# A new order of work inside the pipelined loop of a two-layer gated cross-attention kernel

## The reference

```
x += tanh(g_x[0]) * attention_A(layernorm(x), ctx, mask)   # one head of 256 over ctx, 1601 rows; softmax over 1601
x += tanh(g_f[0]) * mixture_B(layernorm(x))                # router picks 4 of 16 heads of 64; self-attention over 512
x += tanh(g_x[1]) * attention_C(layernorm(x), ctx, mask)   # 16 heads of 16 over the same 1601 rows of ctx
x += tanh(g_f[1]) * experts_D(layernorm(x))                # each row goes to 1 of 8 experts, 256 -> 1024 -> 256
```

## Time and profile before

| | |
|---|---|
| median of 3 runs | 3290.82 us (3289.27 to 3303.54) |
| the profiled execution, its own time | 3308.77 us |
| its span, first to last instruction | 3307.0 us |
| PE busy | 2877.2 us, 87% |
| DVE busy | 1719.2 us, 52% |
| ACT busy | 1459.8 us, 44% |
| granted clock of PE, mean | 0.937 |

### The profile page before, as it was taken

How to read it: one execution, slowest core, us unless ns; L and a number is a source line. 1 busy time by engine, 2 the same in 40 slices (tenths; PEclk the granted TensorE clock), 3 DMA queues, 4 the chain that set the end, 5 groups by cost and what they waited for, 6 DMA issues and landing times.

```text
span 3307.0 us, 38212 instructions
## 1 busy us (share of the span) xinstructions
PE 2877.2 (87%) x13236; PEld 1331.4 (40%) x13236; DVE 1719.2 (52%) x4156; ACT 1459.8 (44%) x2794; POOL 316.6 (10%) x364
## 2 busy tenths in 40 slices
PE   5758988998899888998899889988998888859997
PEld 3423423353334333443344334433343322148886
DVE  1335556556555656555655565555555676621111
ACT  2122454545454555445454545454545555612221
POOL 0110001010100100010101010101010000012221
PEclk7878998999899999999999999998999999969999
DMA  4124212322232214220323032303221121026665
GB/s 156 54 70 110 56 34 77 88 61 50 70 94 55 64 36 119 55 74 28 99 69 80 16 119 62 82 20 119 63 63 33 53 55 36 8 90 220 219 208 175
DMA packets 190687, 267.58 MB, mean 81 GB/s; under 512 B 47813, under 2 KB 159661, under 8 KB 190358
## 3 DMA queue, kind: packets, MB, share of 16 engines
q1 hardware_dynamic: 173084, 189.97, 21.3%
q0 software_dynamic: 17408, 75.13, 6.7%
HBM read 203.24 MB, written 65.61 MB: 81 GB/s over the span
## 4 chain that ended last, share of the span: by engine, by line
PE 72%; DVE 15%; ACT 5%; issue 4%; SPq 3%; DMA 1%; POOL 0%; ACTq 0%; POOLq 0%; DVEq 0%
PE PS L1233 12%; PE PS L1184 10%; DVE mxC L1655 9%; PE PS L1216 7%; PE PS L953 6%; PE PS L929 5%; PE PS L1344 5%; PE PS L1355 5%; PE PS L1019 2%; PE PS L1099 2%; PE PS L1036 2%; PE PS L1029 2%; PE PS L976 2%; DVE nmB L1494 1%; PE PS L940 1%
## 5 line engine op out<-in xcount | busy, mean ns | idle before, releaser
L860 ACT ACTIVATE reg<-PS 128x512 f32<-128x512 f32 (+1 forms) x1664 | 970.3, 598 | 1205.2 <-PE PS L1216 1201.9
L1655 DVE TENSOR_REDUCE mxC<-PS 128x1 f32<-128x400 f32 (+1 forms) x2048 | 1090.1, 569 | 752.9 <-PE PS L1184 743.2
L1184 PE MATMUL PS<-reg 96*128 96x400 bf16 (+1 forms) x2048 | 693.0, 351 | 176.5 <-DVE mxC L1655 155.7
L1216 PE MATMUL PS<-reg 99*128 99x512 bf16 (+1 forms) x1664 | 642.5, 396 | 32.5 <-ACT reg L860 27.1
L1184 PEld LDWEIGHTS PS<-reg 96*128 96x128 bf16 x2048 | 203.1, 99 | 725.0 <-DVE mxC L1655 598.9
L1233 PE MATMUL PS<-reg 128*17 128x512 f32 (+1 forms) x3328 | 461.8, 628 | 0.0
L1216 PEld LDWEIGHTS PS<-reg 99*128 99x128 bf16 (+1 forms) x1664 | 165.6, 102 | 348.5 <-ACT reg L860 159.1
L929 PE MATMUL PS<-reg 128*128 128x512 f32 (+1 forms) x512 | 206.0, 526 | 1.2 <-ACT reg L756 0.7
L883 ACT ACTIVATE reg<-PS,reg 128x256 f32<-128x256 f32 x184 | 77.3, 471 | 271.0 <-PE PS L1344 271.0
L953 PE MATMUL PS<-reg 128*128 128x512 f32 (+1 forms) x416 | 193.1, 598 | 0.4 <-ACT reg L728 0.4
L1344 PE MATMUL PS<-reg 128*128 128x256 f32 x736 | 165.4, 382 | 0.9 <-DVE reg L1815 0.9
(11 more groups left out here) (202 smaller groups left out, 2614.7 us busy)
## 6 DMA issues: line engine op xcount, KB each, us to landing
reg<-in_D_W SPq DMA_DIRECT2D x46, 1024.0 KB, 7.5
reg<-in_A_mask POOLq DMA_DIRECT2D x32, 800.5 KB, 4.8
dramK<-reg SPq DMA_DIRECT2D x144, 100.0 KB
dramV<-reg SPq DMA_DIRECT2D x48, 272.0 KB, 2.1
reg<-in_ctxT POOLq DMA_DIRECT2D x8, 1601.0 KB, 8.3
reg<-in_ctx POOLq DMA_DIRECT2D x8, 1536.0 KB, 8.1
dramQ<-reg SPq DMA_DIRECT2D x96, 128.0 KB
reg<-dramQ SPq DMA_DIRECT2D x32, 384.0 KB, 5.8
```

The lines of the kernel that those rows point to most:

```text
L860: act.activation(pr[u % RING][0:r, :], PS[0:r, s_bank(g, v), :], ACT.Exp).then_inc(a_expC, 1)
L1184: last = mm(PS[:, bank, 0:w], qs[(NG * bb + g) % 3][0:ROWS, h, t * P:(t + 1) * P], ks[g % 2][0:ROWS, h, c0:c0 + w], start=True, stop=True)
L1216: last = mm(PS[0:r, bank, :], ks[g % 2][0:STK, h, c * P:c * P + r], qs[(NG * b + g) % 3][0:STK, h, :], start=True, stop=not with_mask)
L1655: v.tensor_reduce(mxC[:, h, t, j:j + 1], PS[:, MB[i % 2], 0:M_CH[j][1]], AX.X, ALU.max).then_inc(v_mx, 1)
```

## The change

It alters no arithmetic and no number of matmuls, and moves the work between steps and banks.

1. A table, `PIECES`, one digit for each step of a group, says how many pieces (0 to 3) stand in it. `chunks` reads it.
2. The pieces of a step no longer stand first and last: after `scores_t`, after `values_c` of v >= 7, inside many filler parts (between the two halves of a projection) and after each part, `piece()` issues the next one, if there is one left. DVE does the same between its parts.
3. `transpose_m` writes to the maxima bank `MB[0]`. `scores_t` no longer waits for `copy_rows`, and the first piece of the next group does.
4. The projections of keys and of values of C alternate, one of each every four steps, from step 34 to 62 in opposite banks; half of the keys had stood at steps 124 to 133.
5. In stage B, `max_b`, `exp_b` and `normalise` take one tile a step, the pitch of `score_b` goes from four steps to five, and `weigh_b` is split over two steps.
6. In stage A, the layer norm and `turn_x` (`U_XA`) go from 151 to 77, `project_qg` to 136, the scores from 164 to 141, and all sixteen transposes end at step 196 (four stood in steps 2 to 8 of the next period). `weigh_a` issues one matmul a step in 26 steps, where it issued three in every second step.
7. The queries of C (`U_QC`) go from 136 and 138 to 150 and 152; other parts move by a few steps. The transfers move with them.

```diff
-FIRST, LAST = (3, 3, 3, 5), (43, 43, 43, 44)
-U_PV = [10 + 2 * i for i in range(10)]
-U_O1, U_O2, U_OA = (11, 13), (15, 17), (30, 32)
-U_XD, U_GATE = (31, 33), 36
-U_V = [34, 36, 38, 40, 42, 45, 47]
-U_XB, U_RL = (44, 46), 50
-U_K = [52, 56, 60, 64, 124, 127, 130, 133]
-U_QB, U_KB, U_VB = (70, 71), (73, 74), (76, 77)
-U_SB = [80 + 4 * k + 2 * (k >= 4) for k in range(8)]
-U_TB = [U_SB[i // 2] + (5, 7)[i % 2] for i in range(16)]
-U_PVB, U_OB, U_XC, U_QC = (101, 119), (121, 122), (132, 134), (136, 138)
-U_XA, U_QG = (151, 153), (155, 157)
-U_S = [164, 166, 168, 170, 174, 176, 178, 180, 187, 189, 191, 193, 199, 201, 203, 205]
-U_T = [175, 177, 179, 181, 185, 188, 190, 192, 198, 200, 202, 204, 2, 4, 6, 8]
+PIECES = ("0002213322232323311211210113121301010112001300000000",
+          "0003003312230132102331233323111111031002110100000000",
+          "0001001211031002110222133323330021330113312300000000",
+          "0000000022222213311121322213311121221122111220000000")
+U_O1, U_O2, U_LD, U_XD, U_GATE = (7, 10), (13, 16), 18, (27, 30), 33
+U_OA, U_LB, U_XB, U_RL = (29, 31), 34, (43, 46), 50
+U_K, U_V = [34 + 4 * i for i in range(8)], [35 + 4 * i for i in range(7)]
+U_QB, U_KB, U_VB = (66, 68), (70, 72), (74, 76)
+U_LA, U_XA = 68, (77, 80)
+U_SB = [79 + 5 * k + 3 * (k >= 4) for k in range(8)]
+U_TB = [U_SB[i // 2] + 6 + 2 * (i % 2) for i in range(16)]
+U_PVB, U_OB, U_LC = (U_SB[3] + 11, U_SB[7] + 11), (132, 133), 135
+U_QG, U_XC, U_QC = (136, 138), (143, 146), (150, 152)
+U_S = [141, 144, 147, 149] + [154 + 12 * t + d for t in range(3) for d in (0, 3, 6, 8)]
+U_T = [U_S[4 * t + 3] + 4 + 2 * j for t in range(QT) for j in range(4)]
+U_PV = [199 + 13 * c // 10 for c in range(2 * CT)]
...
 def chunks(g, v):
-    first, last = FIRST[g], LAST[g]
-    upto = [min(max(-(-NSC * (w - first + 1) // (last - first + 1)), 0), NSC) for w in (v - 1, v)]
+    upto = [sum(int(d) for d in PIECES[g][:w]) for w in (v, v + 1)]
     return range(*upto)
...
-            def project_qg(n, LA, m):
+            def project_qg(n, LA, m, piece):
...
                     last = mm(PS[:, FB[m], :], gA[:, k, m * P:(m + 1) * P], xT[:, k, :],
                               start=k == 0, stop=k == KD - 1)
+                    if k == 0:
+                        piece()
...
             def scores_c(bb, g, i, with_mask):
                 h, t, j = chunk(i)
                 if i == 0:
+                    past(pe, a_mrow, NG * bb + g)
...
-                    last = tr(PS[0:3 * GH, bank, t * P // 2:(t + 1) * P // 2].bitcast(BF16),
+                    last = tr(PS[0:3 * GH, MB[0], t * P // 2:(t + 1) * P // 2].bitcast(BF16),
...
-                if v == MT[g]:
-                    pe.wait_ge(a_expC, U)
-                elif v == MT[g] + 1 and (g < NG - 1 or ab):
-                    pe.wait_ge(a_mrow, NG * b + g + 2)
-                else:
-                    past(pe, a_expC, U - 1)
+                past(pe, a_expC, U - 1)
...
+                todo = iter(ahead)
+                def piece():
+                    for i in todo:
+                        scores_c(nb, ng, i, with_mask)
+                        break
+                piece()
...
-                    if u == 153:
+                    if u == U_QC[1] + 8:
                         store_q(n, 1)
...
-            def max_b(n, k):
-                for h in range(2):
-                    i = 2 * k + h
+            def max_b(n, i):
...
-                for k in range(8):
-                    if u == U_SB[k] + 1:
-                        max_b(n, k)
-                    if u == U_SB[k] + 3:
-                        normalise(n, k)
+                for i in range(16):
+                    if u == U_SB[i // 2] + 1 + i % 2:
+                        max_b(n, i)
+                        piece()
+                    if u == U_SB[i // 2] + 4 + i % 2:
+                        normalise(n, i)
+                        piece()
```

More of the change, by code:

```diff
@@ L830, in start_next @@
                         evac_qg(m, k)
-                for i in range(12):
+                for i in range(16):
                     if u == U_T[i] + 1:
@@ L836, in start_next, with copy_rows @@
                         exp_a(m, t)
[L838 removed]
+            def copy_rows(bb, g):
                 act.wait_ge(pe_mT, NG * bb + g + 1)
[L840 removed]
+                act.activation(mrow[:], PS[0:3 * GH, MB[0], 0:S // 2].bitcast(BF16), ACT.Copy).then_inc(a_mrow, 1)
             def evac_o(bb, g):
@@ L893, in _, with nothing @@
             FB = (F0, F1)
+            def nothing():
+                pass
             pe.wait_ge(ld["a"], 16)
@@ L950, in weigh_a, with out_a @@
                     pe.wait_ge(v_ttr, 16 * n + 16)
-                for c in range(3 * j, min(3 * j + 3, CT)):
-                    r = rows(c)
-                    last = mm(PS[:, FB[m], :], ctxN[0:r, c, m * P:(m + 1) * P], ptA[0:r, c, :],
-                              start=c == 0, stop=c == CT - 1)
-                if j == 4:
+                r = rows(c)
+                last = mm(PS[:, FB[m], :], ctxN[0:r, c, m * P:(m + 1) * P], ptA[0:r, c, :],
+                          start=c == 0, stop=c == CT - 1)
+                if c == CT - 1:
                     last.then_inc(pe_otA, 1)
-            def out_a(n, j):
+            def out_a(n, j, piece):
                 pe.wait_ge(a_otA, 2 * n + 2)
@@ L985, in route, with project_b @@
                 last.then_inc(pe_rl, 1)
-            def project_b(n, m, which):
+            def project_b(n, m, which, piece):
                 if which == 0:
@@ L1030, in turn_b, with weigh_b @@
                 last.then_inc(pe_tB, 1)
-            def weigh_b(n, p):
-                pe.wait_ge(a_ptB, 16 * n + 8 * (p + 1))
-                for k in range(QT):
+            def weigh_b(n, p, half):
+                if half == 0:
+                    pe.wait_ge(a_ptB, 16 * n + 8 * (p + 1))
+                for k in (2 * half, 2 * half + 1):
                     for h in range(2):
@@ L1037, in weigh_b, with out_b @@
                                   ptB[h][:, k, :], start=k == 0, stop=k == QT - 1)
-                last.then_inc(pe_pvB, 1)
-            def out_b(n, j):
+                if half:
+                    last.then_inc(pe_pvB, 1)
+            def out_b(n, j, piece):
                 pe.wait_ge(v_otB, 2 * n + 2)
@@ L1157, in prepare, with start_next @@
                         turn_b(n, i)
-            def start_next(m, u):
+                        piece()
+            def start_next(m, u, piece=nothing):
                 for k in range(KD):
@@ L1163, in start_next @@
                         turn_x(norm_a(m), k)
+                        piece()
                     if u == U_QG[k]:
-                        project_qg(m, norm_a(m), k)
+                        project_qg(m, norm_a(m), k, piece)
+                        piece()
                 for i in range(16):
                     if u == U_S[i]:
-                        score_a(m, i)
-                for i in range(12):
+                        score_a(m, i, piece)
+                        piece()
+                for i in range(16):
                     if u == U_T[i]:
                         turn_a(m, i)
+                        piece()
+                if u in U_PV:
+                    weigh_a(m, U_PV.index(u))
+                    piece()
             def scores_c(bb, g, i, with_mask):
@@ L1255, in step @@
                 if v == MT[g] and 0 <= nb < B:
-                    past(pe, a_expC, NU * b + u - 1)
-                    transpose_m(nb, ng, SB[((UN + 1) * g + MT[g]) % 2])
+                    transpose_m(nb, ng)
                 if 0 <= b < B:
-                    scores_t(b, g, v, nb < B, with_mask)
-                for i in ahead[:1]:
-                    scores_c(nb, ng, i, with_mask)
+                    scores_t(b, g, v, with_mask)
+                todo = iter(ahead)
[3 more added lines that the diff above has]
+                        break
+                piece()
                 if 0 <= b < B:
@@ L1283, in step @@
                     mm(PS[:, F1, 0:TE * NE], onesD, ohf, start=True, stop=True).then_inc(pe_rank, 1)
-                for i in ahead[1:]:
+                for i in todo:
                     scores_c(nb, ng, i, with_mask)
```

263 lines of the change are left out of this document (156 added, 107 removed).

## The result

The kernel with the change takes 3142.96 us (median of 4 runs, 3137.79 to 3146.23) against 3292.14 us for the kernel before on the same chip (4 runs). The ratio is 0.954, with a 95% interval of 0.951 to 0.957: faster by 149 us.

A forecast was written before the change was run, and what follows sets the result against it. PE's in-order list with local shortages was taken as the bound. Terms gave 23.4 us a period, 140 for six, plus 15 - 4 + 18 = 169 us: 3308.8 to 3140, median 3120 us (3060 to 3170, chance 0.62).

The forecast's parts named there:

- clock and tails: PE's busy time: less work at the low clock level, 5.5 us a period; fewer exposed matmul ends, 4 us.
- Pieces, keys and single tiles: PE's waits on maxima: piece order 3.7 us a period, stage B one tile a step 4.4, keys interleaved with values 1.5.
- the term for the rate: PE's pieces outrunning DVE's maxima: the new order leaves 8.2 of 11.9 us, a gain of 3.7 a period.
- Stage B's chain: Transposes and `weigh_b` get a step more behind their inputs: 6 us a period back, less 2 for ACT's load.
- Rows of maxima, and the exponentials: Rows in the maxima bank and `exp_a` out of the period's last step end waits on exponentials: 2.3 us a period.
- Queries: First piece at step 164 waits for the later query load: 2 us late, up to 8 with shared bandwidth; 2 charged.
- (a): Rival, chance 0.17: new waits take half, with queries 8 us late; the gain falls 12 us a period, to 3205 us.
- Before the first sequence: Fillers ahead of the loop: PE's waits for heads' weights and layer norms shrink, 18 of 28 us (8 to 28).
- the norm for sequence 1 is done 70 steps early: Fillers before the first sequence: the early norm was part of the reason for taking back 18 of 28 us.
- (b): Rival, chance 0.05: nothing gained, PE's waits only change names and become waits on ACT; 3275 us.
- (c): Rival, chance 0.07: many short waits keep PE's clock low in stage B and thin steps; 3620 us, or 3340 in part.
- (d): Rival, chance 0.09: all waits and the low clock level go, 39 us a period; from 2990 us up.

The follow-up runs named there:

- the even spread: Kernel after, but with the pieces of a group spread evenly over the same steps in place of the table: 3165.58 us, ratio 0.961.
- the queries first: Kernel after, with group 0's query load directly behind its store, ahead of the keys, and group 1's query load at step 172: 3104.53 us, ratio 0.942.
- the version at 3101 us: Kernel after, with group 0's query load ahead of the keys and stage B's tiles in pairs at pitch five: 3101.41 us, ratio 0.942.

## Why the prediction held, point by point

**The total.** The working gave 169 us from the profiled execution, and the trace has 164.0. The profiled execution after took 3144.8 us, forecast 3140. The larger part of the miss of 23 us is the step from that execution to the median: 18 us lay between them before and were carried over, but only 1.8 lie between them after (3144.8 and 3143.0). Of the trace's 164 us, 147 came in six periods (140 forecast) and 5 before the first sequence (18 forecast): the misses have opposite signs, +7 and -13, and that they offset in part is luck.

**The period.** The sum said 23.4 us, and 24.2 were found. So close a hit is partly luck, since terms miss in opposite directions: waits were to give 13.9 us and gave 10.9, clock and tails were to give 9.5 and gave 13.4.

- *Pieces, keys and single tiles* were to take 3.7 + 4.4 + 1.5 = 9.6 us of the 19.4 of waits on maxima. They took (97.0 - 29.8) / 5 = 13.4. Too small was the term for the rate, 3.7. It took both orders' lists as PE and DVE would run them, and judged the table, the places in a step and the new steps as one thing. The runs part them, in one order of adding: pieces between parts 18 us, single tiles 60 more, all moved steps and banks 53 (3219 to 3166), the table 23. The order matters: taken away last, pieces between parts cost 89. The steps of the table hold up to three pieces; with only two places in a step, the second and third stand on end, each waiting for a maximum of 0.57 us. The trace shows the stalls that follow; that three in a bunch are what makes the places dear there is inferred, since no run varies the number in a bunch alone.
- *Stage B's chain.* 6 us were to come back on its transposes, less 2 on ACT. `turn_b` and `weigh_b` gave back 38.4 - 19.5 = 18.9 over five periods, 3.8 and not 6. `turn_b` still waits for `evac_pb` twenty times, up to 1.7 us. Single tiles gave 68 us on the kernel before, about the sum in size (4.4 + 6 - 2 = 8.4 a period, 59 in seven), but by another way: the waits like the 1.11 shrank to 0.52 and did not go, those on maxima, `turn_b` and `weigh_b` gave 4.7 a period, and the clock about as much again. In the new order single tiles give nothing. That the pitch of five and the pieces between parts have already made the room is likely and not shown, since no run takes those away beside them.
- *Rows of maxima, and the exponentials.* A gain of 2.3 was forecast for the end of the waits on exponentials. They rose from 2.3 to 3.3 (16.3 / 5), and it is the table that makes them: in the even spread they are 1.1 (5.5 / 5). The bank itself gives 2 us in all, not 14, and with the old bank back they stay at 3.1 (15.7 / 5): in the new order the drain of `MT[g]` is not what PE waits for. In the kernel before, one of the four, 1.3 us, stood at the period's start, as the prediction says of `exp_a`, and in sequence 3 it is gone.
- *Split maxima.* Not foreseen: `transpose_m` in step `MT[g]` waits 2.4 us a period for DVE's `split_m`. `split_m` needs all 64 maxima of its group and stands behind a step's pieces and parts on DVE, and the table keeps pieces dense until shortly before it; with pieces bunched at the end it grew to 4.7. In the even spread it is 1.0.
- *Queries.* 2 us were charged; 4.2 came as waits, and 4.9 of time hung on them. In sequence 3 the wait was 5.2 us, past the 5 that the prediction had named as a sign that it would be wrong (3.7 to 5.2 in the five periods). The sign came and the total held all the same, because the maxima and the clock gave more than their terms. The projection and the store were timed rightly. The landing was taken from a median of 5.8 us, and took 8.7 among the transfers that the new order put beside it. Both causes were named, the loads ahead in SP's list and bandwidth that is shared, but gave the second a price only in rival (a).
- *Clock.* This is the term that was most mis-sized: 5.5 us were forecast, with 4 for tails, and busy time fell by 13.4. The prediction assumed that PE works for some half of the time at the low level. It works for nearly all of it: in the five periods of the kernel before, the stretches at 0.50 add to 150 us with PE busy for 142, in those of the kernel after to 34 with 30 busy. One of them, before:

```profile
1530.20:1537.00 6.80, 6.80 (x24) 2.54 (x25) 1.06 (x4) 2.57 (x5) 0.00 (x0) 0.50 0.02 4
```

So 22 us of PE's work a period moved from the lower level to the upper one, and at 1.91 us against 1.02 for the same matmuls that gives back 10 to 11 us, twice the term; some 2 to 3 of the 13.4 are left for tails. The whole loss before was 14 us a period (half of 142 / 5) and not 9; the 17 us that the prediction set beside its own sum were nearer. Groups 1 and 2, taken to keep a part of the low level, lost all of it.

**Around the periods.** Sequence 6 gave 15.9 (15 forecast) and the last sequence cost 4.0 (4 forecast). Before the first sequence 18 were forecast and 5 came. PE's timeline there, its three longest waits behind the first 30 us:

```profile
148.42 3.78 PE L1005 MATMUL PS<-reg 128*128 128x512 f32 x4 [5.33 <-DMA bs<-in_B_b]
157.53 3.37 PE L1005 MATMUL PS<-reg 128*128 128x512 f32 x4 [5.33 <-DVE reg L1535]
175.21 1.12 PE L913 MATMUL PS<-ident,reg 128*128 128x128 f32 x4 [7.42 <-DVE reg L1462]
```

The 12.9 us for the heads' weights became two waits of 5.3 of stage B's projections: for the fetch (`bs`), and for DVE to read the eighth key's bank (L1535), which the forecast had named as the place behind the fetch. The 6.5 and 8.7 for norms became one of 7.4 for the norm of stage A (L913), whose user moved ahead with it; the step that failed is "the norm for sequence 1 is done 70 steps early": early against its user's old place. So 10 of the 28 us came back. A new wait took 4 of them, before a score of A, on nothing that the profile names:

```profile
251.10 3.75 PE L937 MATMUL PS<-reg 128*128 128x512 f32 x4 [4.03 <-issue]
```

What it waits for stays open.

**The signs.** Of those that the prediction named, the period (319.8 for about 320), the clock in groups 1 and 2 (1.00) and the last sequence (4.0 longer) came. Waits on maxima are 6.0 us a period and not 11, those of `turn_b` and `weigh_b` 3.9 and not under 2, and the stretch before the first sequence takes 313 and not 300.

**The rivals.** (a), new waits take half, was right in its mechanism and small in its effect: SP's one list and shared engines made the queries late, 39 us of the 84 that it wanted. (b) is out: idle and busy time both fell. (c) is out: in five periods there were 102 waits on maxima alone, none over 0.5 us, and groups 0 to 2 of sequence 3 kept 1.00; the clock fell only in or just behind the five waits for the queries. The rule of the Trainium skill ("TensorE: Matmul & The Clock Gate", A second HAM failure mode) that was weighed there, of short idles that swing the level, is not seen at waits of this length. But a wait need not be as long as 3.7 to 5.2 us. With the queries first, the clock fell four times in the five periods, three of them just behind this wait of `turn_b`:

```profile
1405.67 0.77 PE L1039 MATMUL PS<-ident,reg 128*128 128x128 f32 x4 [1.72 <-ACT reg L754]
```

The same wait stands in every period of the kernel after, and no fall follows it there. In the kernel before, the clock also fell at 1598.5, behind waits of 1.23, 0.52 and 0.98 us. (d), all of the waits and the low level gone, did not come: even the version at 3101 us, whose clock is 1.00, keeps 20 us of idle time a period.

## What to carry to other kernels

When an operation is moved later, its transfer is priced among the transfers that will then run beside it, not by its usual landing time; and the needed load goes first in its engine's list. On an in-order engine, first look for what stands on end: short pieces that each wait for another engine are best put between the parts of long work, and how much that brings depends on how they are bunched. Price edits of one order together and then test them both ways, alone on the old kernel and taken from the new one: here one was worth 68 us alone and nothing in the end, and another 18 alone and 89 in the end.

## What the runs showed of the hardware

A transfer of 384 KB took 3.7 us to land with the engines at 0.40, 4.3 when it was issued ahead of its neighbours, 6.4 behind three loads of keys, and 8.7 behind these and one more of queries, beside a mask and a store. Over the period the transfer engines were busy 0.27 of the time, but 0.88 while this one ran. A mean share says little of one transfer. TensorE's granted clock held at its upper level (2.4 GHz) through stretches with many waits of up to 0.5 us, and fell to the lower one (1.2 GHz) in or just behind each of five waits of 3.7 to 5.2 us. Behind waits of 1.7 us it sometimes fell and sometimes did not. With the wait for the queries gone and those of `turn_b` down to 1.0 it was 1.00, rounded, over five periods, at 93% busy. A mean clock near 1 hides much: at a mean of 0.96, PE did 142 of its 1547 us at the lower level, and nearly all of that time was work, so a wait that lets the clock fall costs more than its own length.
